# Row maxima of the scores carried by single-number transfers instead of a TensorE turn and a ScalarE copy

## What is computed

```python
q = jnp.einsum('bsd,hdk->bhsk', x, w_q)
k = jnp.einsum('bsd,hdk->bhsk', x, w_k)
v = jnp.einsum('bsd,hdk->bhsk', x, w_v)
scores = jnp.einsum('bhqk,bhmk->bhqm', q, k) * scale
weights = jax.nn.softmax(scores, axis=-1)
z = jnp.einsum('bhqm,bhmk->bhqk', weights, v)
```

## Time and profile before

| | us |
|---|---|
| median of 3 runs | 1506.01 (1503.9 to 1507.67) |
| the profiled execution | 1504.45 |
| its span, first to last instruction | 1502.5 |
| mean granted clock of PE, share of full | 0.992 |
| PE busy in the span | 1477.6 |
| POOL busy | 1217.7 |
| DVE busy | 995.6 |
| ACT busy | 784.0 |

### The profile page before, as it was taken

One profiled execution on the slowest core, in us unless ns is written; L12 is line 12 of the kernel. 1 busy time (PEld: TensorE's weight loads), 2 busy tenths in 40 slices (PEclk: granted clock), 3 DMA queues, 4 the chain that ended last, 5 costly groups with the idle time before them and its releaser, 6 DMA issues.

```text
span 1502.5 us, 21668 instructions
## 1 busy us (share of the span) xinstructions
PE 1477.6 (98%) x7240; PEld 840.9 (56%) x7240; DVE 995.6 (66%) x1222; ACT 784.0 (52%) x1540; POOL 1217.7 (81%) x676
## 2 busy tenths in 40 slices
PE   8999999999999999999999999999999999999897
PEld 5455555555555555555555555555555655555586
DVE  6557666676767656666666666676667766777543
ACT  4465555555555555555555555565554555544331
POOL 5888779898798878988788878889789998899645
PEclk9999999999999999999999999999999999999899
DMA  6334444432444434333344443334444334340431
GB/s 146 84 86 98 92 114 101 115 93 59 93 100 93 115 83 94 86 79 84 86 107 101 97 94 78 85 86 93 95 96 101 89 72 102 92 107 23 133 84 34
DMA packets 125293, 137.88 MB, mean 92 GB/s; under 512 B 44106, under 2 KB 69197, under 8 KB 125184
## 3 DMA queue, kind: packets, MB, share of 16 engines
q1 hardware_dynamic: 118784, 130.26, 37.3%
q0 software_dynamic: 2048, 4.10, 0.9%
q10 hardware_dynamic: 4352, 2.13, 0.5%
HBM read 16.81 MB, written 8.45 MB: 17 GB/s over the span
## 4 chain that ended last, share of the span: by engine, by line
PE 88%; POOL 5%; DVE 3%; issue 1%; ACT 1%; SPq 1%; DMA 1%; POOLq 0%; ACTq 0%; DVEq 0%
PE ps_w L1391 27%; PE ps_w L1375 16%; PE ps_w L1376 14%; PE ps_m L1323 10%; POOL acc L662 4%; PE ps_m L1424 3%; PE ps_w L1409 2%; PE ps_m L1291 2%; PE ps_m L1292 2%; PE ps_m L1293 2%; PE ps_w L1698 1%; PE ps_m L1698 1%; PE ps_m L1308 1%; PE ps_m L1309 1%; PE ps_m L1310 1%
## 5 line engine op out<-in xcount | busy, mean ns | idle before, releaser
L662 POOL TENSOR_TENSOR acc<-acc,ring 128x1024 f32<-128x1024 f32 x383 | 920.8, 2404 | 50.3 <-ACT ring L831 2.3
L1063 DVE TENSOR_REDUCE mxw<-ps_m 128x1 f32<-128x1024 f32 x512 | 601.8, 1217 | 324.1 <-PE ps_m L1323 321.1
L831 ACT ACTIVATE ring<-ps_w 128x512 f32<-128x512 f32 x1024 | 544.3, 600 | 251.6 <-PE ps_w L1376 236.4
L1391 PE MATMUL ps_w<-ring,V 128*64 128x512 f32 x2048 | 467.7, 598 | 0.0
L1375 PE MATMUL ps_w<-queriesA,keysA 128*128 128x512 f32 x1024 | 431.6, 422 | 2.7 <-issue 1.4
L1376 PE MATMUL ps_w<-queriesB,keysB 65*128 65x512 f32 x1024 | 406.4, 397 | 0.0
L1391 PEld LDWEIGHTS ps_w<-ring,V 128*64 128x64 f32 x2048 | 135.7, 136 | 265.5 <-issue 236.1
L662 POOL TENSOR_TENSOR acc<-ring 128x1024 f32<-128x1024 f32 x64 | 152.2, 2377 | 158.9 <-PE ps_w L1409 150.6
L1375 PEld LDWEIGHTS ps_w<-queriesA,keysA 128*128 128x128 f32 x1024 | 193.6, 189 | 103.5 <-issue 48.7
L1376 PEld LDWEIGHTS ps_w<-queriesB,keysB 65*128 65x128 f32 x1024 | 194.4, 190 | 33.6 <-issue 0.7
L1323 PE MATMUL ps_m<-keysA,queriesA 64*128 64x512 f32 x1000 | 183.0, 444 | 0.9 <-DVE mxw L1063 0.6
(11 more groups left out here) (185 smaller groups left out, 985.5 us busy)
## 6 DMA issues: line engine op xcount, KB each, us to landing
queriesA<-qk_high SPq DMA_DIRECT2D x248, 128.0 KB, 2.4
keysB<-qk_high SPq DMA_DIRECT2D x124, 128.0 KB, 2.4
keysA<-qk_rest SPq DMA_DIRECT2D x124, 128.0 KB, 2.4
queriesB<-qk_rest SPq DMA_DIRECT2D x124, 128.0 KB, 2.4
by_sums<-sums SPq DMA_DIRECT2D x240, 64.0 KB, 2.0
keysA<-qk_high SPq DMA_DIRECT2D x93, 128.0 KB, 2.4
tokens_by_slot<-blank ACTq DMA_DIRECT2D x16, 130.0 KB, 3.2
ring<-tokens_by_slot SPq DMA_DIRECT2D x8, 260.0 KB, 5.3
```

The costliest lines, as they stand in the source:

```text
L662: pool.tensor_tensor(acc[h][:, :], before, P_both(kt), ALU.add).then_inc(summed, 1)
L831: act.activation(P_tile(kt, p), ps_s[k % 3][:, :], ACT.Exp, scale=SCALE).then_inc(exp_done, 1)
L1063: dve.tensor_reduce(mxw[h][:, p * HT + qt:p * HT + qt + 1], ps_m[p][:, :], AX_X, ALU.max).then_inc(maxed, 1)
L1391: mm = pe.matmul(ps_z[p * DK:(p + 1) * DK, :], V_of(j, kt, p), P_tile(kt, p), start=(kt == 0), stop=(kt == KT - 1))
```

## The change

DVE writes the maxima rounded (`mxw` is of type fp32r) and SP carries them from the column into the row itself: for each head and each tile of 128 queries one transfer of 128 single numbers, from [128 partitions, 1] to [1 partition, 128]. So `place_max` has eight issues in place of two, and waits on DVE's `maxed`. PE's transposes, ACT's copies, `mxt`, `c_turned` and `c_copied` go, and with them the wait of PE on `c_copied`. DVE waits on `c_placed` before it overwrites `mxw[h]`. Each half counts 128 on `c_placed` (eight times 16) instead of 32.

```diff
-        mxw = [sb(f"mxw{i}", [P, 2 * HT]) for i in range(2)]
-        mxt = [sb(f"mxt{i}", [2 * HT, P], F32R) for i in range(2)]
+        mxw = [sb(f"mxw{i}", [P, 2 * HT], F32R) for i in range(2)]
...
             def place_max(j, par, h):
-                sp.wait_ge(c_copied, 2 * j + h + 1)
+                sp.wait_ge(maxed, 8 * (2 * j + h) + 8)
                 for p in range(2):
-                    sp.dma_start(queriesB[par][p][DK:KC, h * HALF:(h + 1) * HALF].bitcast(F32)
-                                 .rearrange("o (t q) -> o t q", q=P),
-                                 mxt[h][p * HT:(p + 1) * HT, :].bitcast(F32)).then_inc(c_placed, 16)
+                    for t in range(HT):
+                        at = h * HALF + t * P
+                        sp.dma_start(queriesB[par][p][DK:KC, at:at + P].bitcast(F32),
+                                     mxw[h][:, p * HT + t:p * HT + t + 1].bitcast(F32)).then_inc(c_placed, 16)
...
-            def copy_max(j, h, bank):
-                act.wait_ge(c_turned, 2 * j + h + 1)
-                act.activation(mxt[h][:, :], bank[0:2 * HT, 0:P], ACT.Copy).then_inc(c_copied, 1)
...
-                    if oct == 1:
-                        copy_max(j, 1, lent_max)
-                    if oct == 3 and not last:
-                        copy_max(j + 1, 0, lent_max)
...
                         if oct in (1, 3) and not (first and oct == 1):
-                            dve.wait_ge(c_turned, 2 * j + (1 if oct == 1 else 2))
+                            dve.wait_ge(c_placed, 128 * (2 * j + (1 if oct == 1 else 2)))
...
-            def turn_max(j, h, bank):
-                pe.wait_ge(maxed, 8 * (2 * j + h) + 8)
-                pe.transpose(bank[0:2 * HT, 0:P], mxw[h][:, :], ident[:, :]).then_inc(c_turned, 1)
...
                 if k == 0 and oct % 2 == 0:
-                    pe.wait_ge(c_placed, 32 * (2 * j + h) + 32)
+                    pe.wait_ge(c_placed, 128 * (2 * j + h) + 128)
...
-                    if oct == 1:
-                        turn_max(j, 1, lent_max)
-                    if not last and oct == 3:
-                        turn_max(j + 1, 0, lent_max)
...
-                        if oct in (1, 3):
-                            pe.wait_ge(c_copied, 2 * j + 2 + oct // 2)
```

More of the change, by code:

```diff
@@ L187, in block_kernel @@
         maxed = sem("maxed")
-        c_turned = sem("c_turned")
-        c_copied = sem("c_copied")
         c_placed = sem("c_placed")
@@ L898, in _ @@
             cast_qk(1, 1, 0)
-            copy_max(0, 0, ps_z)
             in_order(act, pair)
@@ L1647, in _ @@
             pe.wait_ge(first_copied, 4)
-            turn_max(0, 0, ps_z)
             first_visit(4, 0)
```

## The result

The changed kernel takes 1694.86 us (median of 4 runs, 1684.15 to 1701.38) against 1504.95 us for the kernel before on the same chip: a ratio of 1.1256, 95% interval 1.1223 to 1.1289. It is 190 us slower. The direction was forecast, and so were two of the three losses, the wait at h = 1 and the fall of the clock behind it; the third, in octet 0, was put at nothing. 1634 was said, and the range ended at 1690.

A forecast was written before the change was run, and what follows sets the result against it. TensorE was taken to bound the kernel, busy 1477.6 of 1502.5 us. 1504.45 + 84 (wait at h = 1) + 3 (lead-in) + 48 (clock) - 7 (transposes) = 1632.5, adjusted to 1634 for the runs' median; range 1550 to 1690.

The forecast's parts named there:

- wait at h = 1: TensorE ahead of octet 2, pairs 0 to 30: waits 2.7 us each for the second half's maxima, 84 us.
- fall of the clock: TensorE's clock after the new waits: 28 of 32 bring one fall of 1.7 us, 48 us; bounds 0 and 109.
- first half's eight issues, octet 0: First half's maxima (h = 0): arrive at 632.8, wanted at 634.33, so covered by 1.5 us, cost nothing.
- lead-in: First half of pair 0: maxima there at 32.4, wanted at 29.89, a 2.5 us wait; 3 us rounded up.
- transposes: 64 transposes removed from TensorE, 0.11 us each: 7 us gained, at most 17.
- cover there is at h = 1: Second half's maxima: 3.86 us mean from first issue to scores; today's two transfers need 2.4, leaving 1.3 in hand.
- Pitch 0.64 us, 2.0 us to arrive: SyncE's eight issues: last starts 4.48 us after the first, lands 2.0 later; maxima there after 6.48 us.
- priced it only as a rival: Slow transfers at twice the pitch, 1.28 us, supported by one 1.80 us issue: 1870 to 1931 us, chance 0.09.
- So this is covered, with 0.2 us in hand.: Place of use 0, shifted 1.6 us behind the first half's issues: VectorE ends at 638.9, PE's visit comes at 639.11.
- VectorE's wait for `c_placed` costs nothing: VectorE's new wait, replacing `c_turned`, is for transfers TensorE already waited for half a pair before: nothing.
- Rivals: Clock holds 1586 (0.18), short issues 1567 (0.11), slow transfers 1870 to 1931 (0.09), faster 1499 (0.04), no change 1506 (0.02).
- The signs: Profile after: eight-issue runs of 5.1 us, PE idle 2.7 us ahead of octet 2 once a pair, clock 0.96 to 0.97.

The follow-up runs named there:

- e1_order: Changed kernel with SyncE issuing the second half's eight maxima transfers ahead of the place of use 3 instead of behind it: 1533.27 us, ratio 1.0181.
- e5b: Changed kernel with TensorE kept busy by 12 unused products of the identity during its wait ahead of octet 2: 1631.96 us, ratio 1.0849.
- e9: e1_order with two of the first half's eight issues moved from SyncE to ScalarE's queue, pair 0 included: 1506.96 us, ratio 1.0008.
- e8: e9 with the old way (turn, copy, two transfers) kept for the first half of pair 0 alone: 1502.52 us, ratio 0.9971.
- e3_eight_rows: Kernel before, turn and copy kept, with eight transfers of 128 side-by-side numbers in place of two of 512: 1756.81 us, ratio 1.1685.
- e2_strided: Changed kernel with visits taking every fourth query, so two issues fill a half instead of eight: 1530.92 us, ratio 1.0168.

## Why the prediction was wrong, point by point

The experiments make a staircase: 1694.9, with the clock held up 1632.0, with the second half's wait gone too (and the filling with it) 1533.3, with the first half's queue relieved 1507.0, with the lead-in mended 1502.5. Each against the kernel before on its own chip, the steps are 64, 98, 27 and 4 us.

| term of the sum | forecast | measured |
|---|---|---|
| wait at h = 1, pairs 0 to 30 | 84 | 95 (31 waits of the trace over the usual gap; octets 1, after against e1_order) |
| fall of the clock | 48 | 63 (after to e5b) |
| first half's eight issues, octet 0 | 0 | 33 (octets 0 of pairs 1 to 31, after against before); 27 come back from e1 to e9, 24 of them in octets 0 |
| lead-in | 3 | 5 with its fall of the clock (after against before, to the end of octet 0 of pair 0); 4 (e9 to e8) |
| transposes | -7 | -8 (octets 1 and 3, e1 against before) |

- *What bounds, and what cover there is at h = 1.* Right. The distance from first issue to scores, 3.86 us in the mean of 31 pairs, read from the timeline, was the number on which everything rests, and e1_order shows it from the other side: give the eight issues their 5 us and the wait is gone.
- *Pitch 0.64 us, 2.0 us to arrive.* Right for most pairs and short in the mean. In pair 13 it is 5.12 us for eight and 6.59 us in all, for 6.48. But in eight of the 31 pairs one of the eight issues lasts 1.33 to 1.82 us, and the last of the eight starts 5.24 to 5.72 us after the first instead of 4.50. The mean of all 31 is 4.78, and from the first issue to PE 6.86 us. PE would have come after 3.80 us, for the 3.75 of the forecast. So the wait is 3.06 us on average rather than 2.7, and the 11 us by which the term was short are mostly the long issues. The earlier trace rows had one of 1.80 us; I priced it only as a rival. What makes an issue long no run tells.
- *The clock.* The mechanism was right: a wait of 3 us brings a fall in most pairs, in 27 of 31 for the 28 forecast; a gap of 3.29 us in pair 4 brought none. The term was mis-sized in the price of a fall: I took 1.7 us from one place in the lead-in, and 63 us over 27 falls is 2.3 us each. From the mean clock, (1 - 0.940) x 1692.8 = 102 us are lost against 12 before, but part of that was spent idle.
- *"So this is covered, with 0.2 us in hand."* This step failed: it is the 33 us. The shift itself came out near the forecast: `wst` starts 8.0 us into octet 3 on average against 6.3 before, 1.7 us later for the 1.6 of the sum. In pair 13 it is 1.9, from 5.99 us (629.76, octet 3 from 623.77) to 7.88 (octet 3 from 714.94). 0.3 us of that is `by_sums`, which starts later behind a VectorE that is late in octet 2; e1_order takes this away (there `wst` starts at 7.57), and octet 0 keeps its excess. SP's queue in the timeline after:

```profile
712.05 5.02 SPq L496 DMA_DIRECT2D by_sums<-sums  x8
717.12 0.58 SPq L421 DMA_DIRECT2D wo<-in_L_attn_w_o  x1
717.74 5.03 SPq L485 DMA_DIRECT2D queriesB<-mxw  x8
722.82 0.59 SPq L404 DMA_DIRECT2D wst<-in_L_attn_w_q  x1
```

  What was wrong is that I followed the shift into VectorE's queue only. The cast on ScalarE waits for the same buffer, and behind the cast in ScalarE's order stand the exponentials of units 3 and 4, for which PE waits. In octet 0 that cast stands idle for 0.92 us on average, against 0.11 in the kernel before, 0.94 in e1_order and 0.24 in e9_split_only. ScalarE, PE and PE's visit in the next octet 0, and last PE's same load in the kernel before:

```profile
728.24 0.60 ACT L768 ACTIVATE qk_high<-ps_m 128x512 fp32r<-128x512 f32 x1 [0.41 <-DMA keysB<-qk_high]
...
729.38 0.19 PEld L1361 LDWEIGHTS ps_w<-queriesA,keysA 128*128 128x128 f32 x1 [0.65 <-ACT ring L826]
...
730.54 0.30 PEld L1313 LDWEIGHTS ps_m<-keysA,queriesA 64*128 64x128 f32 x4 [0.37 <-DVE qk_rest L1044]
...
637.97 0.19 PEld L1375 LDWEIGHTS ps_w<-queriesA,keysA 128*128 128x128 f32 x1 [0.29 <-ACT ring L831]
```

  Behind the 0.41 us on ScalarE PE idles for 0.65 us where it idled for 0.29, and the octet is 0.36 us longer. The visit, for which the forecast had its 0.2 us of margin, shows its usual gap of 0.37 us: the path that was priced costs nothing here. Over pairs 1 to 30 PE's idle time in octets 0 has grown by 18.6 us ahead of those scores (the seventh unit) and by 3.6 us ahead of the visit, so most of the loss came by the path that was not priced. The long ones of these waits also bring the clock down. This is pair 1 of e1_order, a load of the scores and the stretch behind it:

```profile
85.10 0.19 PEld L1363 LDWEIGHTS ps_w<-queriesA,keysA 128*128 128x128 f32 x1 [2.56 <-ACT ring L828]
...
85.00:90.00 5.00, 4.90 (x16) 2.07 (x18) 2.41 (x3) 4.30 (x11) 0.05 (x1) 0.66 0.90 201
```

- *VectorE's wait for `c_placed` costs nothing.* Right, though the view of waits seems to say otherwise: 43.5 us, 29 times. Look at one, and at PE's visit ahead of it, after and then before:

```profile
720.50 0.30 PEld L1313 LDWEIGHTS ps_m<-keysA,queriesA 64*128 64x128 f32 x4 [0.36 <-issue]
...
721.33 2.36 DVE L1053 TENSOR_REDUCE mxw<-ps_m 128x1 fp32r<-128x1024 f32 x2 [1.44 <-DMA queriesB<-mxw]
...
629.42 0.30 PEld L1323 LDWEIGHTS ps_m<-keysA,queriesA 64*128 64x128 f32 x4 [0.37 <-issue]
...
630.26 2.36 DVE L1063 TENSOR_REDUCE mxw<-ps_m 128x1 f32<-128x1024 f32 x2 [1.55 <-PE ps_m L1323]
```

  The reduction starts 0.83 us after the visit, in the kernel before 0.84 us. A landing of the first half's eight transfers, on the same semaphore, fell into that time and was named as the releaser. e1_order has 57.2 us of such waits at octets of the old length.
- *The rule of the Trainium skill* (DMA: Bandwidth & Descriptors, Rules for kernel authors) that single numbers become a descriptor each and a rearranged transpose is 19 times slower: the first half agrees with the trace (packets under 512 B rise from 44106 to 117322); of the second nothing is seen, for landing stays at 2.0 us and e3_eight_rows is slow without any single number. No run here has the hardware's own transpose in a transfer to set beside it, so the factor itself is not tested.
- *Rivals and range.* None of the rivals happened. The range had room above the forecast for a later arrival (12 us) and for second falls of the clock (44), which covers what these two terms were short by, 11 and 15. It had no room for octet 0, which was short by 33.
- *The signs.* PE idles ahead of octet 2 once in each pair, as said, and not at a pair's start but for pair 0. The clock over the span is 0.940, below the 0.96 to 0.97 that was said.

The step from e5b_spin12 to e1_order is 99 us, while the waits in the trace sum to 95 over the usual gap. Octets 1 are 100 us longer in e5b_spin12 than in e1_order (95 in the kernel after) and octets 2 are 3 us longer, while the end of the kernel is 4 us shorter: 5 of the 100 are the filling's own cost, and the 3 go with a VectorE that is late in octet 2, argued and not tested.

What stays open: what makes some issues last over 1 us, and why a product of `z` on VectorE lasts 1.30 us in pair 13 of the kernel before and 2.79 us after; no run separates it. And of the 33 us in octets 0 the waits account for 22; how the rest divides between falls of the clock behind them and other things no run tells, for none holds the clock up in octet 0.

## What to carry to other kernels

Count transfers in issues, not in bytes or pieces: most took 0.64 us of their queue here, a few over 1 us, and what matters is what stands ahead of it and behind it in that queue. Before replacing a turn on an engine by transfers, measure the distance from the first issue to the consumer, and if eight issues don't fit, try their place in the queue first; one reordering regained 162 of 190 us. And when a step shifts a queue, price the shift in every engine that waits for what stands behind, since the shortest margin decides. An idle gap of TensorE of some 3 us cost its length here, and in 27 of 31 places the clock too.

## What the runs showed of the hardware that was not expected

- A weight load whose 128 columns stand four numbers apart took 317 ns instead of 184 (e2_strided, 1000 loads). Octets 1 and 3 are 0.25 us longer than in e9_split_only, which also has neither transposes nor waits there, but no stride.
- Transfers of 128 single numbers, from 128 partitions into one, landed in 2.0 us (512 of them, 1.9 to 4.2), the same as the median of `by_sums`, 64 KB each.
- TensorE waiting 3 us for data cost 5 us: 3 for the wait and 2 for the clock behind it. 24 small matmuls with no use, in the gap, gave the 2 us back.
